# Two-layer graph network on one core: earlier tables and gathers at the start, layer 1's table fetch in eight pieces instead of seven

## The reference

```
layer 0 (attention):
  h = x @ W;  a_src = h @ att_src;  a_dst = h @ att_dst
  e = leaky_relu(a_src[src] + a_dst[dst], 0.2)      (edges, and one loop per node)
  alpha = softmax of e over the edges of each dst
  x = layernorm(x + tanh(segment_sum(h[src] * alpha, dst) + bias))
layer 1 (messages):
  h = gelu(x @ W_pre + b_pre)
  x2 = x + segment_sum(h[src] * edge_attr, dst)
  out = layernorm(x + x2 + gelu(gelu(x2 @ W1 + b1) @ W2 + b2))
```

## Time and profile before

| | before |
|---|---|
| median of 3 runs | 3898.72 us (3898.11 to 3900.5) |
| profiled execution, its own time | 3902.33 us |
| its span, first to last instruction | 3900.5 us |
| PE, DVE, ACT, POOL busy | 2459.8, 2440.5, 1260.4, 2788.1 us |
| chain that ended last, by engine | PE 36%, POOL 21%, issue 16%, DVE 13%, ACT 8% |

### The profile page before, as it was taken

The page is one execution under the profiler, slowest core; times in us unless marked ns, Lnnn a source line. Parts: engine busy times, 40 slices in busy tenths (PEclk is TensorE's granted clock), DMA queues, the critical chain, the costliest instruction groups (busy, mean ns, idle before and its releaser), DMA issues.

```text
span 3900.5 us, 66528 instructions
## 1 busy us (share of the span) xinstructions
PE 2459.8 (63%) x16652; PEld 1997.6 (51%) x16653; DVE 2440.5 (63%) x6233; ACT 1260.4 (32%) x3759; POOL 2788.1 (71%) x2950
## 2 busy tenths in 40 slices
PE   5433343434344444444438999898888888888886
PEld 3333333333333333333336777776676666666665
DVE  7444444444566666666657777766777777767765
ACT  4333343434455555555542111111111111121112
POOL 6777777777777777777747777776776666666664
PEclk7555555555555555555559999999988989899887
DMA  4222222222222222222233444343343333333332
GB/s 88 43 42 42 42 43 42 43 42 44 44 43 44 44 43 44 44 43 43 45 76 87 90 95 91 88 94 86 87 90 85 85 85 85 85 80 87 82 85 55
DMA packets 350815, 254.00 MB, mean 65 GB/s; under 512 B 253985, under 2 KB 278386, under 8 KB 350555
## 3 DMA queue, kind: packets, MB, share of 16 engines
q0 software_dynamic: 94016, 146.16, 19.3%
q1 hardware_dynamic: 241144, 99.08, 11.0%
q10 hardware_dynamic: 15394, 6.42, 0.7%
HBM read 244.10 MB, written 7.25 MB: 64 GB/s over the span
## 4 chain that ended last, share of the span: by engine, by line
PE 36%; POOL 21%; issue 16%; DVE 13%; ACT 8%; DVEq 2%; ACTq 2%; DMA 2%; POOLq 0%; SPq 0%
PE bank L921 29%; POOL rows L623 21%; PE bank L907 5%; ACT onehot L675 4%; DVE hot L1261 3%; DVE node L1278 2%; DVE score L1160 1%; ACT pair L695 1%; ACTq L668 1%; DMA rows<-table,src_i 1%; DVEq L1077 1%; DMA src_i<-in_src_dram 1%; ACT L768 1%; ACTq L706 1%; DVE newp L1151 1%
## 5 line engine op out<-in xcount | busy, mean ns | idle before, releaser
L623 POOL DMA_INDIRECT rows<-table,src_i x2890 | 2733.6, 946 | 1073.2 <-issue 869.6
L921 PE MATMUL bank<-node,hot 128*128 128x288 bf16 x9310 | 1263.6, 299 | 57.6 <-DVE hot L1261 41.7
L921 PEld LDWEIGHTS bank<-node,hot 128*128 128x128 bf16 x9310 | 945.4, 103 | 338.3 <-issue 55.0
L857 PE MATMUL bank<-onehot,rows 128*97 128x72 f32 (+1 forms) x3136 | 601.4, 369 | 786.6 <-ACT onehot L705 784.5
L857 PEld LDWEIGHTS bank<-onehot,rows 128*97 128x97 f32 x3136 | 545.8, 281 | 827.1 <-issue 762.1
L1261 DVE TENSOR_SCALAR hot<-node,key 128x642 bf16<-128x642 int16 x1862 | 864.1, 539 | 156.2 <-PE bank L921 84.2
L907 PE MATMUL bank<-onehot,rows 128*96 128x72 f32 (+1 forms) x3136 | 343.9, 273 | 161.0 <-DVE acc L1298 161.0
L907 PEld LDWEIGHTS bank<-onehot,rows 128*96 128x96 f32 x3136 | 334.5, 187 | 177.7 <-DVE acc L1298 141.2
L774 ACT ACTIVATE pair<-dst_i 128x8 f32<-128x8 int32 x196 | 35.2, 180 | 1191.8 <-DVE rows L1295 1187.1
L675 ACT ACTIVATE onehot<-iota,far_dst 128x72 f32 (+1 forms) x1568 | 385.3, 328 | 23.4 <-ACT far_dst L672 0.7
L1139 DVE SCALAR_TENSOR_TENSOR other<-onehot,bank 128x576 f32<-128x576 f32 (+1 forms) x196 | 121.8, 621 | 429.8 <-ACT bank L688 308.4
(11 more groups left out here) (167 smaller groups left out, 1938.9 us busy)
## 6 DMA issues: line engine op xcount, KB each, us to landing
attr<-in_edge_attr_dram SPq DMA_DIRECT2D x190, 336.0 KB
rows<-table,src_i POOLq DMA_INDIRECT x2890
node<-in_src_dram SPq DMA_DIRECT2D x190, 64.0 KB
attr<-in_edge_attr_dram SPq DMA_DIRECT2D x190, 48.0 KB
src_i<-in_src_dram SPq DMA_DIRECT2D x200, 4.0 KB
dst_i<-in_dst_dram SPq DMA_DIRECT2D x200, 4.0 KB
src_i<-in_src_dram SPq DMA_DIRECT2D x190, 3.5 KB
dst_i<-in_dst_dram SPq DMA_DIRECT2D x190, 3.5 KB
```

What stands on the lines that cost most here:

```text
L623: pool.indirect_dma_start(rows[:, u, j * width:(j + 1) * width], None, table, bass.IndirectOffsetOnAxis(ap=src_i[:, u, j:j + 1], axis=0))\
L857: last = pe.matmul(total[:, 0:w], rows0(u)[:, j, 0:D1], wide(weights, w)[:, j, :], start=j == 0, stop=j == TILES - 1)
L921: last = pe.matmul(p_got[t], hot[:, c % HOTS, i, t * P:(t + 1) * P], tab[:, a, :, :].rearrange("p k d -> p (k d)"), start=a == 0, stop=a = ...
```

## The change

- **Front.** The tables of windows and due chunks and `score_column(0)` are made inside DVE's chunk loop, after chunks 6, 8 and 10 (PE's matmuls for them after chunks 5 and 7). ACT makes `given(0)` before `away(1)`. SP loads the source indices of round 1 into a tile of their own, `src_next` (five DMAs ahead of the weights), and POOL gathers round 1 into a tile of its own, `rows_next` (it lies over `hot`, which the front uses for `zcol`), so its gathers wait only for the stored table and the end of the chunk loop (`a_peak`). Rounds 0 and 1 of layer 0 are written out ahead of the loop (`alone=2`).
- **Layer 1, pieces.** The 49 blocks are cut into eight pieces, seven of 6 blocks and one of 7. PE fetches pieces 0,1; 2,3; 4; 5; 6,7 behind u = 0 to 4, the last two behind the node chunk's `final`. DVE marks 0,1; 2,3; 4; 5,6; 7, but from round 1 on piece 0 is marked at the head of the round's first message, before its wait for `feed`.
- **Layer 1, taking.** At u = 0 the product of the seven gathered tiles comes first; then the first fetched tile alone is summed and multiplied, which gives `e1_msg`; then the other four are summed, and then `acc` is added. `g_out` counts twice a round.
- **Layer 1, indices.** SP loads the fetched tiles' source numbers at u = 0 of the round instead of u = 2, and ACT shortens them to 16 bits at the end of u = 4 (before ACT's part of `final`) instead of at the head of u = 0.

```diff
@@ sizes
-        ERA = NB // PART
+        ERA = 8
+        PIECE = [NB * c // ERA for c in range(ERA + 1)]
+        rows_next = hot[...].bitcast(FP32)[:, 0:SLOTS * TILES * D2].rearrange("p (u e) -> p u e", u=SLOTS)
+        AT_LINES, AT_WINDOWS, AT_DUE, AT_SCORE = 5, 6, 8, 10
...
-        def era(it, u):
...
-            starts = [-(-k * ERA // SLOTS) for k in range(SLOTS + 1)]
-            return range(starts[u], starts[u + 1])
+        MARKED = ((0, 1), (2, 3), (4,), (5, 6), (7,))
+        FETCHED = ((0, 1), (2, 3), (4,), (5,), (6, 7))
@@ SP
+            for u in range(SLOTS):
+                sp.wait_ge(e0.src[u], 16)
+                sp.dma_start(src_next[:, u, :], src[...]).then_inc(e0.src[u], 16)
...
-                if u == 2 and len(era(it, u)):
+                if u == 0 and it is not ROUNDS:
                     load_booked_src(it)
@@ POOL
                         if u == SLOTS - 1:
                             pool.wait_ge(a_st, 16 * CHUNKS)
+                            pool.wait_ge(a_peak, CHUNKS + RING)
+                        return
+                    if e is e0 and second(it):
+                        pool.wait_ge(e.rows[u], 16 * TILES)
+                        for j in range(TILES):
+                            pool.indirect_dma_start(rows_next[:, u, j * width:(j + 1) * width], None, table, ...)
@@ ACT
+            def shorten_src(it):
+                act.wait_ge(g_src, 16 * BOOKED * (it + 1))
+                if not first(it):
+                    act.wait_ge(g_hot, it * ERA)
+                act.activation(src16[:, :, 0:ROW3], src_all..., ACT.Copy).then_inc(g_src16, 1)
             def ahead(g, it, u, ws):
-                if u == 0 and len(era(it, u)):
...
                 if g is not LAST:
                     feed(g + 1, it + (u + 1) // SLOTS, (u + 1) % SLOTS)
+                if u == SLOTS - 1 and fetching(it):
+                    shorten_src(it + 1)
@@ PE
                 if c == 0:
-                    pe.wait_ge(g_out, it + 1)
-                for i in range(PART):
+                    pe.wait_ge(g_out, it * 2 + 1)
+                for i, a in enumerate(range(PIECE[c], PIECE[c + 1])):
...
-                for c in era(it, u):
-                    fetch(it, c)
+                    for c in FETCHED[u]:
+                        fetch(it, c)
@@ DVE
-            every_chunk((2, rows_made), (1, spans_at), (0, peaks))
-            score_column(0)
+            every_chunk((2, rows_made), (1, spans_at), (0, peaks), (0, tables_at))
...
-                v.wait_ge(g_done, it * ERA + max(c - HOTS + 1, 0) + 1)
+                if not first(it) or c >= HOTS:
+                    v.wait_ge(g_done, it * ERA + c - HOTS + 2)
...
+                if u == 0 and fetching(it) and not first(it):
+                    marks(it, 0)
                 v.wait_ge(e1_fed, g + 1)
...
-                    if u == 0:
-                        taken(it)
-                    v.wait_ge(g_out, it + 1)
...
+                product = v.tensor_tensor(rows[:, u, 0:cut], rows[:, u, 0:cut], p_attr[:, 0:cut], ALU.mult)
+                if booked(it, u) and u == 0:
+                    taken(it, range(1))
+                    v.wait_ge(g_out, it * 2)
+                    v.tensor_tensor(rows[:, u, cut:TILES * D], got[:, u, :], p_attr[...], ALU.mult).then_inc(e1_msg, 1)
+                    taken(it, range(1, BOOKED))
+                else:
+                    product.then_inc(e1_msg, 1)
```

More of the change, by code:

```diff
@@ L297, in gnn @@
         h_zero = sem("h_zero")
[L298 removed]
+        h_in = sems("h_in", ERA - 1)
         h_hi = sem("h_hi")
@@ L378, in one @@
                     after_round(it)
-            if first_round:
-                one(0, SLIM, SLIM)
-            with eng.Fori(int(first_round), SLIM_ROUNDS - 1) as it:
+            for it in range(alone):
+                one(it, SLIM, SLIM)
+            with eng.Fori(alone, SLIM_ROUNDS - 1) as it:
                 one(it, SLIM, SLIM)
@@ L443, in gathered1, with fetching, piece @@
             return 16 * ((TILES - 1) * it + TILES)
-        def era(it, u):
-            if it is ROUNDS or it is ROUNDS - 1:
-                return range(0)
-            starts = [-(-k * ERA // SLOTS) for k in range(SLOTS + 1)]
-            return range(starts[u], starts[u + 1])
+        def fetching(it):
+            return it is not ROUNDS and it is not ROUNDS - 1
+        MARKED = ((0, 1), (2, 3), (4,), (5, 6), (7,))
+        FETCHED = ((0, 1), (2, 3), (4,), (5,), (6, 7))
+        def piece(c):
+            return slice(PIECE[c], PIECE[c + 1])
         class Steps:
@@ L620, in body @@
                             pool.wait_ge(a_st, 16 * CHUNKS)
+                            pool.wait_ge(a_peak, CHUNKS + RING)
[3 more added lines that the diff above has]
+                        for j in range(TILES):
+                            pool.indirect_dma_start(rows_next[:, u, j * width:(j + 1) * width], None, table,
+                                                    bass.IndirectOffsetOnAxis(ap=src_next[:, u, j:j + 1], axis=0))\
+                                .then_inc(e.rows[u], 16)
                         return
@@ L797, in _ @@
             feed(0, 0, 0)
-            groups(act, ahead, lambda it: due(act, it, final), first_round=True)
+            groups(act, ahead, lambda it: due(act, it, final), alone=1)
             rest(act, final)
@@ L1312, in message @@
                         v.wait_ge(x1_v, before + k + 1)
-                for c in era(it, u):
-                    (split_and_mark if first(it) else marks)(it, c)
+                if fetching(it):
+                    for c in MARKED[u]:
+                        if first(it):
+                            split_and_mark(it, c)
+                        elif c > 0:
+                            marks(it, c)
                 if g is not LAST:
```

203 lines of the change are left out of this document (114 added, 89 removed).

## The result

| | before | after |
|---|---|---|
| median | 3899.6 us (3898.11 to 3901.54, 4 runs) | 3840.5 us (3838.08 to 3842.84, 4 runs) |
| profiled execution, its own time | 3902.33 us | 3842.3 us |
| its span | 3900.5 us | 3840.5 us |
| POOL waiting for indices in layer 1 | 128.2 us, 40 times (2100 to 3850 us) | 85.3 us, 21 times (2080 to 3800 us) |

The ratio is 0.9849, with a 95% interval of 0.9834 to 0.9865: 59 us faster, where 46 were forecast (3852, range 3805 to 3886).

What follows compares the result with a forecast made beforehand. POOL's pace was taken to bound layer 0 and the PE - DVE chain layer 1. The terms -18.6 - 6 - 26 + 5 = -46, subtracted from the median of 3898.7, gave 3852 us, range 3805 to 3886.

Steps and rivals of the forecast that it cites:

- The front, -18.6: Layer 0: POOL's first gather out of the table moves from 79.5 to 60.9 us, all of it arriving at layer 0's end.
- The step on round 2's first slot: Layer 0: SP's load for round 2 comes some 4 us earlier, without a stall; if no earlier, POOL waits 2.9 us.
- Ahead of the first chunk, 9 x -0.7: Layer 1, nine rounds before any node chunk: POOL's 43.7 us a round binds, -6 us in all.
- Plain rounds behind it, 13 x -2: Layer 1, 13 rounds without a chunk after the first chunk: 42.7 us instead of 44.7, -26 us.
- the straight part: PE's 36 blocks and five sums in a layer 1 round: 28.8 us, or 31.7 with 2.9 us at 1.2 GHz.
- Chunk rounds, 52.5: Layer 1, 15 rounds with a node chunk: 52.5 us against 52.2, +5 us in all.
- The go: DVE's signal for PE to start the chunk: 3.0 us behind the fifth sum instead of 0.9, behind piece 7's marks.
- ACT's copy: 16-bit index copy of 0.74 us, moved ahead of the chunk's Gelu: charged 0.4 us per chunk.
- The function table: ACT's table load behind the copy: 1.28 us by the trace; by the skill's 2.66 us, the total 21 us higher.
- Only the front pays: Rival: late chunk start and low clock leave layer 1 at -10 to +12 us: 3870 to 3892, chance 0.24.
- Clock high and go early: Rival: PE's clock stays high over shorter idle, rounds 39.8 and 48 us, layer 1 gives 80 to 100: 3780 to 3815, chance 0.14.
- The clock low through all 13 blocks: Rival: blocks behind a chunk at 1.2 GHz cost 16 us instead of 9.7, +94 in all: 3946, chance 0.05.

Runs made afterwards that it cites:

- no_next: Changed kernel without the early gathers of round 1, on a chip where engines stood still: 5722.1 us, 1.0247 of the kernel before there.
- add_first: Changed kernel with DVE adding the finished window ahead of the takings at a round's first slot, instead of behind the last: 3771.7 us, 0.9669 of before.
- one_taking_b: Changed kernel with the split of the takings undone, all five fetched tiles taken before the product of slot 0: 3838.9 us, 0.9841 of before.
- dve_copy_b: Changed kernel with the 16-bit index copy made by DVE behind its marks of piece 7, instead of by ACT: 3856.3 us, 0.9879 of before.
- copy_last: Changed kernel with ACT's 16-bit index copy moved behind ACT's part of the node chunk: 3833.0 us, 0.9831 of before.
- one_behind: Changed kernel with one piece of the fetch behind the node chunk instead of two, piece 6 fetched with piece 5: 3849.2 us, 0.9871 of before.

## Why the prediction was right

The mechanisms named for the front, for the rounds ahead of the first chunk and for the plain rounds are the ones that the traces show. In a chunk round the forecast had two of its terms wrong in opposite directions, and that they cancel is luck. In all the sum gave 14 us less than the 60 us by which the spans differ; 9 of them are the plain rounds and 6.5 two stretches that had no term.

**The front, -18.6: right.** First table gather forecast at 60.9, found at 60.69; 18.1 us arrived at layer 1 and nothing stalled in between. The step on round 2's first slot was too timid: I took the load 4 us earlier and it came 10.1 earlier, all of what DVE's first group gained. That the whole gain needs `rows_next` and not only the earlier tables is argued from the trace, not shown (no_next has only the other regime).

**Ahead of the first chunk, 9 x -0.7: right.** 8 rounds at 43.71, against 43.7 forecast: POOL's pace.

**Plain rounds behind it, 13 x -2: mis-sized.** There are 14, at 42.14 instead of 42.7, so -35.3 instead of -26: the largest single error. The boundary took 11.2 us against 11.0, the wait ahead of the sum 2.43 against 2.5, and the reason given for it, the addition behind the takings, is shown by add_first and one_taking_b. Too high was the straight part: 42.14 - 11.23 = 30.9 us, not 31.7. The forecast had charged it with the 2.9 us at 1.2 GHz of the boundary that it had read. In the changed kernel the stretch from a round's first sum to its second (the sum and 60 fetches) takes 10.7 us in the mean of the 14 plain boundaries, 2.0 more than at full clock. At two of them the clock does not fall at all. Here it is granted 1.00 from 3350 to 3362 us, against 0.77 from 3158 to 3173 around the boundary shown above, though the wait is the same 2.43 us:

```profile
3352.90 1.58 PE L947 MATMUL bank<-onehot,rows 128*96 128x72 f32 x16 [2.43 <-DVE acc L1356]
3354.31 7.51 PE L960 MATMUL bank<-node,hot 128*128 128x288 bf16 x60
3361.66 1.50 PE L947 MATMUL bank<-onehot,rows 128*96 128x72 f32 x16
```

The other half of the forecast for a plain round, that PE no longer waits for marks behind its first sum, holds: this wait took 33.4 us in 37 times before (2100 to 3850 us), and 1.8 us in 3 times after (2080 to 3800 us). How much of it is due to the early marks of piece 0 and how much to the smaller pieces is not shown.

**Chunk rounds, 52.5: right in sum, wrong in its parts.** 52.55 us, +7.1 over 15 against +5. The go was taken at 3.0 us behind the fifth sum with "DVE working in order"; it came at 1.08, since an increment without a wait of its own did not wait for the marks ahead of it (3194.77 against 3195.58), and with a wait it did (3.43, dve_copy_b). ACT's copy was charged at 0.4 us and cost 2.3, because it waits for exactly those marks. The two errors cancel, 3.0 + 0.4 against 1.08 + 2.3: the late marks of piece 7 do cost PE some 2 us, only at the Gelu and not at the go. PE's last wait was 3.26 against 2.5, the 65 fetches 9.86 against 9.7.

**The function table.** On the row, ACT's copy ends at 3196.36 and the Gelu starts at 3198.00, 1.64 us with the load of 1.28 in it. The Trainium skill, "ScalarE: Activation LUTs", section "What ACT_TABLE_LOAD costs", gives 2.66 us with its drain; the trace does not bear that out here. The total alone would not decide it, since other terms were off by as much.

**Not priced:** -4.0 us between layer 1's first gather and its first taking, and -2.5 in the tail.

**The rivals.** Only the front pays: no, layer 1 gave 42 us. Clock high and go early: the go was early, the clock stayed high at few boundaries, 2 of the 14 plain ones (granted 0.92 from 2460 to 3780 us, 0.91 before), and ACT took back what the go gave. This rival was also priced too low. Its own rounds of 39.8 and 48 us give 13 x 4.9 + 15 x 4.2 = 127 us, not 80 to 100, and average 44.2 us, above POOL's 43.7, so POOL would not have held them; and 48 has the straight part at the slow clock, at full clock it would be about 45. add_first, where the clock does stay high at the plain boundaries, has 39.63 and 50.46 us and 3771.7 in all, below the rival's 3780. The clock low through all 13 blocks: no, 9.86 us, not 16. POOL's waits in layer 1 were forecast near 90 us and were 85.3. The 8.35 us that the prediction calls the largest wait in the kernel before is an ordinary one behind a chunk (7.2 to 9.5 in that window); nothing in the sum hangs on it.

## What to carry to other kernels

When an instruction is made ready earlier, look at everything else its consumer waits for: here PE needed the product and the freed window, and moving one line, the addition, ahead of the takings gave 69 us, more than the whole change gave, while the split of the takings by itself gave none. In a queue in order, ask of each step that is moved what it waits for and who stands behind it: the copy of 0.74 us cost 2.3 us of another engine's time. An edit that removes one wait has to be followed to the next engine, as dve_copy and copy_last gave all or most of their gain back there, and one_behind much of its loss.

## What the runs showed of the hardware

A DVE semaphore increment without a wait of its own let PE start 0.8 us before the DVE instructions ahead of it had ended (PE at 3194.77, marks until 3195.58). PE starts the chunk 0.9 to 1.3 us behind its fifth sum in all 15 chunks, and 3.3 to 3.5 us behind it in all 15 of dve_copy_b, where a wait and a copy stand ahead of the increment.

After 2.43 us of idle time PE's clock fell at one boundary and not at another (sums of 2.84 and 1.58 us), and over all 14 plain boundaries it fell at twelve; after 0.9 us, in add_first, it fell at none of 14. What decides between the two boundaries with the same wait is not shown.

A Copy on ACT behind a Sqrt had a function table load of 1.28 us ahead of it (copy_last).

On two occasions engines stood still between instructions for reasons that the profile doesn't name, and the kernel before took 43 and 44% longer (5589 and 5616 us) than elsewhere. There the order of the kernels is another: the changed front by itself is 0.7% slower than before, and the four kernels with the changed layer 1 are 2.5 to 3.8% slower, where two of the same kernels are 1.2 and 1.6% faster elsewhere. The kernel before was not profiled there, so the cause of the standstills, and why the new layer 1 suffers more, stay open.
